# Fewer vector operations between the rank products and the places of routed rows, in a two-layer mixture-of-experts and state-space kernel

## The chip, the cores and the metric

The kernel runs on one core of one Trainium2 chip. The metric is the device time of one execution in microseconds (us). The engines are called by the profile's names: PE (TensorE, matrix products; PEld is its weight loads), DVE (VectorE), ACT (ScalarE), POOL (GpSimd) and SP (SyncE, which here only starts transfers).

## What is computed

1024 rows of width 256 (4 sequences of 256) go through three residual blocks: half a mixture-of-experts (MoE) block, a state-space scan, and half the same MoE block again. The MoE block, cut to what matters:

```python
logits = einsum('th,eh->te', xt, w_router)            # 8 experts
scores = sigmoid(logits)
topk_w, topk_i = top_k(scores, 2)                     # two experts for each row
topk_w = topk_w / sum(topk_w)
comb = zeros((T, 8)).at[arange(T)[:, None], topk_i].add(topk_w)
gate = silu(einsum('th,eih->tei', xt, wg)); up = einsum('th,eih->tei', xt, wu)
expert_out = einsum('tei,ehi->teh', gate * up, wd)    # inner width 640
out = einsum('te,teh->th', comb, expert_out)          # + two shared experts (sg, su, sd) for every row
```

The scan has, for each row, 256 channels and 16 states: `h = exp(dt * A) * h + dt * B * x`, `y = h . C + D * x`. All is float32.

## The kernel before

**Segments.** The rows are cut into two halves of 512. The program has four segments: the first MoE block on half 0 and on half 1 (segments 0 and 1), then the second MoE block on half 0 and on half 1 (2 and 3). The scan of half 0 runs between tiles of segment 1, that of half 1 between tiles of segment 2. Every segment has 17 tiles of 128 rows: 8 of the two shared experts (kind "shared"), 5 "whole" tiles for experts 0 to 4 and 4 "mixed" tiles of four groups of 32 rows: one group whose expert is looked up at run time and three of fixed experts (`MIXED`). A tile is gate and up projections (L510 or L525 on PE), tanh on ACT (L784), two DVE operations (L1031, L1035), the down projection (L535 or L548) and, for a shared tile, its addition to the residual on DVE (L1046, tile `xres`). `first(n)` issues the projections of tile n + 1, `second(n)` the down projection of tile n. The projections have two halves of the accumulators in flight: `rest_of_gate_up(n)` waits on `s_ev` until tile n - 2 has been moved out of PSUM, which for a shared tile is L1046.

**Routing.** Only the two best experts of a row compute it. On DVE `route_scores` finds them as one-hot arrays `one1` and `one2` (4 blocks of 128 rows x 8 experts) and adds them into `both`. PE's `rank` multiplies `both` by a triangular matrix (rank of each row within its block, L602) and by ones (totals of the blocks, L603), into PSUM bank 7. DVE's `route_rows` turns these into places: it sums the totals over earlier blocks (L1147), counts the 32-row groups that an expert needs beyond its own room (L1150 to L1158), adds steps and bases and picks the places of the two experts of every row (L1161 to L1172), and writes them as integers to `pos` (L1173, L1174). POOL then scatters the normalized rows to these places in the DRAM buffer `xg_rows` with eight indirect transfers (L957), four and four: the second four wait until the first four have landed. SP loads tiles from there (L391, into `xg`), and PE turns them (L554) on the way to the first whole tile.

**Order.** One table, `SCHEDULE`, is walked by every engine, and each engine runs its own parts in that order. In segment 0 DVE does `route_scores`, the two operations of tile 0, then `route_rows`, and then the two operations of tile 1; segment 0's first whole tile is number 5, and PE turns its rows while it works on tile 3. In segment 1 the step "scored and ranked" stands among the whole tiles; in segments 2 and 3 it stands between shared tiles (32 and 33 in segment 2). In such a step DVE does `route_scores` and `route_rows` back to back, and only then the operations of the next tile and the L1046 of the present one. `link(...)` makes DVE wait for the result of one operation before the next starts; an operation without it may overlap the next.

## Time and profile before

| | before |
|---|---|
| median of 3 runs | 516.63 us (516.49 to 517.44) |
| profiled execution: time, span | 519.28 us, 517.1 us |
| PE busy, instructions | 504.5 us (98%), 4636 |
| DVE busy, instructions | 323.6 us (63%), 650 |
| ACT / POOL busy | 153.9 us (30%) / 229.0 us (44%) |
| granted TensorE clock, mean | 0.997 |
| chain that ended last | PE 81%, DVE 8%, DMA 6%, issue 2%, POOL 2% |

The span is the stretch of the profiled execution in which instructions are recorded. The profile adds 2.2 us around it, and this execution is 2.65 us above the median of the unprofiled runs. "Idle before" an instruction is what its engine lost just ahead of it, with the one that ended the wait; only waits on PE, or on an engine that PE then waits for, touch the end.

### The profile page before, as it was taken

To read this page: it belongs to the slowest core of one execution; us is meant where nothing else is said; L and a number is where in the kernel's file an instruction comes from. 1 tells how busy PE (TensorE), PEld (TensorE's weight loads), DVE (VectorE), ACT (ScalarE), POOL (GpSimd) and SP (SyncE) were. 2 spreads that over 40 slices of the span, in tenths; PEclk is the share of its full clock that TensorE was granted. 3 is DMA by queue.
4 is the path that set the end of the run, shared out by engine and by line. 5 is a ranking of instruction groups with operands and counts; after the bars stand their busy time and mean duration, and the time that the engine had idled before them with its cause. 6 is when DMAs were issued, how large, how long until landed. Compare 5 with 4: busy or idle time off the path is not lost.

```text
span 517.1 us, 11597 instructions
## 1 busy us (share of the span) xinstructions
PE 504.5 (98%) x4636; PEld 420.3 (81%) x4637; DVE 323.6 (63%) x650; ACT 153.9 (30%) x322; POOL 229.0 (44%) x205
## 2 busy tenths in 40 slices
PE   7998999999999999999989999999999999999997
PEld 6998997568979999557889789975598899955796
DVE  3663328222656999998679399999977532422225
ACT  1111132221145444453112634445521111122210
POOL 1042000602315999997353289999930650000032
PEclk9899999999999999999999999999999999999999
DMA  7956999421415556640121534555100231210012
GB/s 226 388 190 248 398 396 350 144 74 31 122 34 135 135 120 157 132 129 20 52 72 43 126 88 130 143 142 153 56 22 3 72 97 57 82 42 15 19 52 82
DMA packets 39639, 64.36 MB, mean 124 GB/s; under 512 B 4864, under 2 KB 22784, under 8 KB 39584
## 3 DMA queue, kind: packets, MB, share of 16 engines
q1 hardware_dynamic: 27264, 36.98, 25.5%
q10 hardware_dynamic: 9088, 18.09, 9.4%
q0 software_dynamic: 3232, 8.53, 5.3%
q8 instruction: 39, 0.64, 0.5%
q14 instruction: 16, 0.13, 0.1%
HBM read 46.93 MB, written 16.65 MB: 123 GB/s over the span
## 4 chain that ended last, share of the span: by engine, by line
PE 81%; DVE 8%; DMA 6%; issue 2%; POOL 2%; SPq 1%; ACT 0%; DVEq 0%; POOLq 0%
PE ps L510 35%; PE ps L535 19%; PE ps L525 14%; PE ps L548 7%; DMA bcb<-bc_rows 2%; PE ps L559 2%; PE ps L554 2%; DMA w_gu<-in_su 1%; DMA xg_rows<-region,pos 1%; POOL xg_rows L957 1%; DMA bc_rows<-hh 1%; PE ps L702 1%; DVE hb L1031 1%; PE ps L593 1%; SPq L368 1%
## 5 line engine op out<-in xcount | busy, mean ns | idle before, releaser
L510 PEld LDWEIGHTS ps<-xnp,w_gu 128*128 128x128 f32 x1280 | 149.0, 193 | 11.6 <-issue 6.2
L510 PE MATMUL ps<-xnp,w_gu 128*128 128x128 f32 x1280 | 152.8, 278 | 4.7 <-DVE xres L1046 3.7
L1031 DVE SCALAR_TENSOR_TENSOR hb<-hb,ps 128x640 f32<-128x640 f32 x68 | 55.5, 816 | 120.2 <-ACT hb L784 120.0
L535 PE MATMUL ps<-w_dn,hb 128*128 128x256 f32 x520 | 120.9, 380 | 0.0
L535 PEld LDWEIGHTS ps<-w_dn,hb 128*128 128x128 f32 x520 | 95.0, 191 | 10.6
L784 ACT ACTIVATE hb<-ps 128x640 f32<-128x640 f32 x68 | 47.6, 700 | 176.8 <-PE ps L510 163.0
L510 PEld LDWEIGHTS ps<-xt,w_gu 128*128 128x128 f32 x800 | 92.4, 192 | 1.1 <-issue 0.2
L510 PE MATMUL ps<-xt,w_gu 128*128 128x128 f32 x800 | 92.8, 276 | 0.0
L1076 DVE TENSOR_TENSOR_SCAN ps<-ps,region 128x512 f32<-128x512 f32 x64 | 78.3, 1223 | 7.9 <-POOL region L995 6.9
L1009 POOL TENSOR_TENSOR xna<-xna,hh 128x512 f32<-128x512 f32 x64 | 81.9, 1282 | 2.0 <-DVE hh L1081 2.0
L975 POOL DMA_INDIRECT region<-yg_rows,pos x32 | 30.7, 959 | 112.2 <-DMA yg_rows<-ob 92.0
L525 PE MATMUL ps<-w_gu,xt 128*32 128x256 f32 (+2 forms) x1024 | 74.5, 434 | 0.0
L957 POOL DMA_INDIRECT xg_rows<-region,pos x32 | 31.5, 986 | 95.2 <-DMA xg_rows<-bcb 40.2
L995 POOL TENSOR_TENSOR region<-region,bcb 128x512 f32<-128x512 f32 x44 | 56.2, 1279 | 19.3 <-DMA bcb<-bc_rows 16.2
L525 PEld LDWEIGHTS ps<-w_gu,xt 128*32 128x32 f32 x1024 | 31.3, 110 | 36.8 <-issue 23.8
L1035 DVE TENSOR_TENSOR hb<-hb,ps 128x640 f32<-128x640 f32 x68 | 55.8, 821 | 3.5 <-PE ps L510 1.2
L878 ACT ACTIVATE ps<-region,aneg 128x510 f32<-128x510 f32 x64 | 43.3, 677 | 0.0
L548 PE MATMUL ps<-w_dn,hb 128*32 128x256 f32 (+1 forms) x640 | 37.6, 380 | 0.0
L811 ACT ACTIVATE ob<-ps 128x256 f32<-128x256 f32 x36 | 13.8, 383 | 68.5 <-PE ps L548 36.0
L548 PEld LDWEIGHTS ps<-w_dn,hb 128*32 128x32 f32 x640 | 20.4, 110 | 13.6 <-issue 0.7
L1081 DVE TENSOR_TENSOR hh<-ps,bcb 128x512 f32<-128x512 f32 x44 | 30.4, 691 | 1.5
L995 POOL TENSOR_TENSOR region<-region 128x512 f32<-128x512 f32 x20 | 25.6, 1280 | 2.7 <-DVE ps L1076 2.7
(110 smaller groups left out, 281.7 us busy)
## 6 DMA issues: line engine op xcount, KB each, us to landing
bcb<-bc_rows SPq DMA_DIRECT2D x22, 512.0 KB, 5.2
region<-bc_rows SPq DMA_DIRECT2D x10, 512.0 KB, 5.4
w_gu<-in_wg ACTq DMA_DIRECT2D x7, 640.0 KB, 8.6
w_gu<-in_wu ACTq DMA_DIRECT2D x7, 640.0 KB, 10.2
w_dn<-in_wd ACTq DMA_DIRECT2D x7, 640.0 KB, 12.9
xg<-xg_rows SPq DMA_DIRECT2D x20, 128.0 KB, 5.0
yg_rows<-ob SPq DMA_DIRECT2D x20, 128.0 KB, 4.3
xg_rows<-bcb SPq DMA_DIRECT2D x1, 2176.0 KB, 13.7
```

The costliest lines, as they stand in the source:

```text
L510: last = nc.tensor.matmul(gup(p)[:, c * P:(c + 1) * P], w_gu4[:, e, k, c * P:(c + 1) * P], x, start=(k == 0), stop=(k == KC - 1))
L525: last = nc.tensor.matmul(gup(p)[r:r + GROUP, a:b], xt[:, p, k, r:r + GROUP], w, start=(k == 0), stop=(k == KC - 1))
L535: ins = nc.tensor.matmul(outp(p), hb[:, p, c * P:(c + 1) * P], w_dn4[:, e, c, :], start=(c == 0), stop=(c == IC - 1))
L548: ins = nc.tensor.matmul(outp(p)[r:r + GROUP, :], hb[:, p, c * P + r:c * P + r + GROUP], w, start=(c == 0), stop=(c == IC - 1))
L784: nc.scalar.activation(hb[:, p, :], gup(p)[:, 0:I], ACT.Tanh, scale=0.5).then_inc(s_tanh, 1)
L878: nc.scalar.activation(bank[:, :, 1:L], dt[:, d, :].rearrange("p (b t) -> p b t", b=2)[:, :, 1:L], ACT.Exp, scale=aneg[:, d * N + m:d * N ...
L957: nc.gpsimd.indirect_dma_start(out=xg_dram[s % 2], out_offset=bass.IndirectOffsetOnAxis(ap=pos[:, s, j, t:t + 1], axis=0), in_=xn["P"][:, ...
L995: nc.gpsimd.tensor_tensor(bx[:, d, :], dtx[:, d, :], bcs[m % SLOTS][:, 0, :], ALU.mult).then_inc(s_bx, 1)
L1009: nc.gpsimd.tensor_tensor(xna[:, d, :], xna[:, d, :], hh[:, d, :], ALU.add).then_inc(s_acc, 1)
L1031: nc.vector.scalar_tensor_tensor(out=h, in0=h, scalar=1.0, in1=gup(p)[:, 0:I], op0=ALU.add, op1=ALU.mult).then_inc(s_a, 1)
L1035: nc.vector.tensor_tensor(h, h, gup(p)[:, I:GU], ALU.mult).then_inc(s_h, 1)
L1076: nc.vector.tensor_tensor_scan(state_banks[:, d, :], state_banks[:, d, :], bx[:, d, :], 0.0, ALU.mult, ALU.add).then_inc(s_scan, 1)
```

## The change

The places are worked out by fewer and larger operations.

- The rows of one expert now lie in one run of `xg_rows` and `yg_rows`: the tiles are laid out in `ROW_ORDER`, so that an expert's whole tile and its groups in a mixed tile are neighbours (`FIRST_ROW`). The step from the first to the later part of an expert (`STEP`) is gone. The rooms, the number of groups and the size of the buffers are the same.
- The sums over earlier blocks and the base of each expert go into the rank products. `both` becomes 8 x 6: per expert a share of the base (1/128 of it in every partition, written once at the start from `plan`), the four blocks, and a zero. One DVE scan over these 48 elements gives `upto`, the running sums per expert (`carry` is 0 at each expert's first element). PE multiplies ones by `upto` (40 columns) and adds the triangular product of `both` (32 columns) into the same bank; 1 is taken from the whole triangular matrix, so that a block's own total is left out again. `s_oh`, for which PE waits, is given by the scan and no longer by the addition ahead of it.
- `route_rows` reads ranks with bases straight from PSUM. The shift of `cum` by one element replaces a subtraction, `one1` and `one2` lie side by side in `tops` and are multiplied, reduced and converted in one operation each. By the rows below it has 11 DVE operations, where it had 25 (four of them the L1147).
- `s_rkc`, which tells PE that bank 7 may be written again, comes after the eighth of these and no longer after the second.
- `ex` is the same buffer as `sc`. The memory that ACT copies zeros from in the scan is `zero8` and no longer `pre`. The constant `plan` has 80 columns, where it had 40.

The diff, cut to its core:

```diff
@@ -23,8 +23,12 @@
 GROUP = 32
 MIXED = [(5, 5, 5), (0, 0, 2), (1, 1, 3), (6, 6, 7)]
 MT = len(MIXED)
-STATIC0 = WHOLE * P
-FREE0 = STATIC0 + MT * 3 * GROUP
+
+ROW_ORDER = [("whole", 0), ("mixed", 1), ("whole", 2), ("whole", 1), ("mixed", 2), ("whole", 3), ("whole", 4),
+             ("mixed", 0), ("mixed", 3)]
+ROW_OWNERS = [e for kind, k in ROW_ORDER for e in ((k,) * 4 if kind == "whole" else MIXED[k])]
+FIRST_ROW = {tile: GROUP * sum(4 if kind == "whole" else 3 for kind, _ in ROW_ORDER[:k]) for k, tile in enumerate(ROW_ORDER)}
+FREE0 = GROUP * len(ROW_OWNERS)
...
-BASE = [P * e if e < WHOLE else STATIC0 + GROUP * OWN.index(e) for e in range(E)]
-STEP = [STATIC0 + GROUP * OWN.index(e) - P - P * e if e < WHOLE and e in OWN else 0 for e in range(E)]
-OVER = [FREE0 - ROOM[e] - BASE[e] - STEP[e] for e in range(E)]
+BASE = [GROUP * ROW_OWNERS.index(e) for e in range(E)]
+OVER = [FREE0 - ROOM[e] - BASE[e] for e in range(E)]
...
-        plan = sb("plan", [P, 5 * E])
-        room, base, step_on, over_on, room_groups = (plan[:, k * E:(k + 1) * E] for k in range(5))
+        plan = sb("plan", [P, 4 * E + E * (TT + 2)])
+        room_end, over_on, end_groups, base_share = (plan[:, k * E:(k + 1) * E] for k in range(4))
+        carry = plan[:, 4 * E:]
...
-        ex = sb("ex", [P, TT, E])
         sc = sb("sc", [P, TT, E])
+        ex = sc
...
-        one1 = sb("one1", [P, TT, E])
...
-        both = sb("both", [P, TT, E])
-        tot = sb("tot", [P, TT, E])
-        pre = sb("pre", [P, TT + 1, E])
-        nt = sb("nt", [P, E])
-        cum = sb("cum", [P, E])
+        tops = sb("tops", [P, 2, TT, E])
+        one1, one2 = tops[:, 0, :, :], tops[:, 1, :, :]
+
+        both = sb("both", [P, E, TT + 2])
+        upto = sb("upto", [P, E, TT + 2])
+        zero8 = sb("zero8", [P, E])
+        nt = sb("nt", [P, E + 1])
+        cum = sb("cum", [P, E + 1])
...
+        m12 = sb("m12", [P, 2, TT])
+        m1, m2 = m12[:, 0, :], m12[:, 1, :]
@@ -383,11 +388,11 @@
...
-                    a, b = FREE0 + m * GROUP, STATIC0 + m * 3 * GROUP
+                    a, b = FREE0 + m * GROUP, FIRST_ROW["mixed", m]
...
-                    a = m * P
+                    a = FIRST_ROW["whole", m]
@@ -598,10 +604,10 @@
             def rank(s):
                 pe.wait_ge(s_oh, s + 1)
                 banks_free()
-                flat = both[:, :, :].rearrange("p t e -> p (t e)")
-                nc.tensor.matmul(bank7[:, 0:TT * E], upper[:, :], flat, start=True, stop=True)
-                nc.tensor.matmul(bank7[:, TT * E:2 * TT * E], ones[:, :], flat, start=True,
-                                 stop=True).then_inc(s_rk, 1)
+                own = both[:, :, 1:TT + 1].rearrange("p e t -> p t e")
+                sums = upto[:, :, 1:TT + 2].rearrange("p e t -> p t e")
+                nc.tensor.matmul(bank7[:, 0:(TT + 1) * E], ones[:, :], sums, start=True, stop=False)
+                nc.tensor.matmul(bank7[:, 0:TT * E], upper[:, :], own, start=False, stop=True).then_inc(s_rk, 1)
                 held[:] = [(s_rkc, s + 1)]
@@ -874,7 +880,7 @@
...
-                    nc.scalar.activation(bank[:, :, 0:1], pre[:, 0, 0:2].rearrange("p (b t) -> p b t", t=1), ACT.Copy)
+                    nc.scalar.activation(bank[:, :, 0:1], zero8[:, 0:2].rearrange("p (b t) -> p b t", t=1), ACT.Copy)
@@ -1120,65 +1126,60 @@
                 link(nc.vector.tensor_scalar(sc[:, :, :], ex[:, :, :], 1.0, None, ALU.add))
                 link(nc.vector.reciprocal(sc[:, :, :], sc[:, :, :]))
...
-                nc.vector.tensor_tensor(both[:, :, :], one1[:, :, :], one2[:, :, :], ALU.add).then_inc(s_oh, 1)
-
-                link(nc.vector.tensor_tensor(kk[:, :], m1[:, :], m2[:, :], ALU.add))
+                link(nc.vector.tensor_tensor(both[:, :, 1:TT + 1].rearrange("p e t -> p t e"), one1, one2,
+                                             ALU.add))
+
+                nc.vector.tensor_tensor_scan(upto[:, :, :].rearrange("p e t -> p (e t)"), carry,
+                                             both[:, :, :].rearrange("p e t -> p (e t)"), 0.0, ALU.mult,
+                                             ALU.add).then_inc(s_oh, 1)
+
+                link(nc.vector.tensor_tensor(kk[:, :], m1, m2, ALU.add))
...
             def route_rows(s):
 
                 dve.wait_ge(s_rk, s + 1)
-                nc.vector.tensor_copy(eq[:, :, :].rearrange("p t e -> p (t e)"), bank7[:, 0:TT * E])
-                nc.vector.tensor_copy(tot[:, :, :].rearrange("p t e -> p (t e)"),
-                                      bank7[:, TT * E:2 * TT * E]).then_inc(s_rkc, 1)
-                dve.wait_ge(s_rkc, s + 1)
-                for t in range(TT):
-                    link(nc.vector.tensor_tensor(pre[:, t + 1, :], pre[:, t, :], tot[:, t, :], ALU.add))
-
-
-                link(nc.vector.scalar_tensor_tensor(out=nt[:, :], in0=pre[:, TT, :], scalar=1.0 / GROUP,
-                                                    in1=room_groups, op0=ALU.mult, op1=ALU.subtract))
-                link(nc.vector.tensor_tensor(needs, nt[:, :].rearrange("p (e a) -> p e a", a=1)
+                rank = bank7[:, 0:TT * E].rearrange("p (t e) -> p t e", t=TT)
+
+
+                link(nc.vector.scalar_tensor_tensor(out=ebase[:, :], in0=bank7[:, TT * E:(TT + 1) * E], scalar=1.0 / GROUP,
+                                                    in1=end_groups, op0=ALU.mult, op1=ALU.subtract))
+                nc.vector.tensor_tensor(eq[:, :, :], rank, over_t(room_end), ALU.is_ge)
+                link(nc.vector.tensor_tensor(needs, ebase[:, :].rearrange("p (e a) -> p e a", a=1)
                                              .to_broadcast([P, E, STEPS]), slots[:, 0:STEPS].rearrange("p (a c) -> p a c", a=1)
                                              .to_broadcast([P, E, STEPS]), ALU.is_gt))
-                link(nc.vector.tensor_reduce(nt[:, :], needs, AX.X, ALU.add))
-                link(nc.vector.tensor_tensor_scan(cum[:, :], ones[:, 0:E], nt[:, :], 0.0, ALU.mult, ALU.add))
-                link(nc.vector.tensor_tensor(ebase[:, :], cum[:, :], nt[:, :], ALU.subtract))
-                link(nc.vector.scalar_tensor_tensor(out=ebase[:, :], in0=ebase[:, :], scalar=float(GROUP), in1=over_on,
+                link(nc.vector.tensor_reduce(nt[:, 1:E + 1], needs, AX.X, ALU.add))
+                link(nc.vector.tensor_tensor_scan(cum[:, :], ones[:, 0:E + 1], nt[:, :], 0.0, ALU.mult, ALU.add))
+                link(nc.vector.scalar_tensor_tensor(out=ebase[:, :], in0=cum[:, 0:E], scalar=float(GROUP), in1=over_on,
                                                     op0=ALU.mult, op1=ALU.add))
-
-                link(nc.vector.tensor_tensor(eq[:, :, :], eq[:, :, :], pre[:, 0:TT, :], ALU.add))
-                nc.vector.scalar_tensor_tensor(out=sc[:, :, :], in0=eq[:, :, :], scalar=P - 0.5,
-                                               in1=over_t(step_on), op0=ALU.is_gt, op1=ALU.mult)
-                link(nc.vector.tensor_tensor(both[:, :, :], eq[:, :, :], over_t(room), ALU.is_ge))
-                link(nc.vector.tensor_tensor(both[:, :, :], both[:, :, :], over_t(ebase[:, :]), ALU.mult))
-                link(nc.vector.tensor_tensor(eq[:, :, :], eq[:, :, :], sc[:, :, :], ALU.add))
-                link(nc.vector.tensor_tensor(eq[:, :, :], eq[:, :, :], both[:, :, :], ALU.add))
-                link(nc.vector.tensor_tensor(eq[:, :, :], eq[:, :, :], over_t(base), ALU.add))
-                nc.vector.tensor_tensor(one1[:, :, :], one1[:, :, :], eq[:, :, :], ALU.mult)
-                link(nc.vector.tensor_tensor(one2[:, :, :], one2[:, :, :], eq[:, :, :], ALU.mult))
-                nc.vector.tensor_reduce(m1[:, :], one1[:, :, :], AX.X, ALU.add)
-                link(nc.vector.tensor_reduce(m2[:, :], one2[:, :, :], AX.X, ALU.add))
-                nc.vector.tensor_copy(pos[:, s, 0, :], m1[:, :])
-                nc.vector.tensor_copy(pos[:, s, 1, :], m2[:, :]).then_inc(s_dest, 1)
+                link(nc.vector.tensor_tensor(eq[:, :, :], eq[:, :, :], over_t(ebase[:, :]), ALU.mult))
+                nc.vector.tensor_tensor(eq[:, :, :], eq[:, :, :], rank, ALU.add).then_inc(s_rkc, 1)
+                dve.wait_ge(s_rkc, s + 1)
+                link(nc.vector.tensor_tensor(tops[:, :, :, :].rearrange("p j t e -> p j (t e)"),
+                                             tops[:, :, :, :].rearrange("p j t e -> p j (t e)"),
+                                             eq[:, :, :].rearrange("p (a t) e -> p a (t e)", a=1).to_broadcast([P, 2, TT * E]),
+                                             ALU.mult))
+                link(nc.vector.tensor_reduce(m12[:, :, :].rearrange("p j t -> p (j t)"),
+                                             tops[:, :, :, :].rearrange("p j t e -> p (j t) e"), AX.X, ALU.add))
+                nc.vector.tensor_copy(pos[:, s, :, :], m12[:, :, :]).then_inc(s_dest, 1)
 
@@ -1201,7 +1202,9 @@
...
             nc.vector.memset(zeros, 0.0).then_inc(s_zero, 1)
-            nc.vector.memset(pre[:, 0, :], 0.0).then_inc(s_boot, 1)
+            nc.vector.memset(zero8[:, :], 0.0).then_inc(s_boot, 1)
+            nc.vector.memset(nt[:, :], 0.0)
+            nc.vector.memset(both[:, :, :], 0.0)
             link(nc.vector.memset(ones[:, :], 1.0))
             nc.vector.memset(rt[:, :], 0.0).then_inc(s_boot, 1)
@@ -1231,6 +1234,8 @@
                     dve.wait_ge(s_aneg, 1)
                 elif kind == "start":
                     copy_logits(0)
+                    dve.wait_ge(s_cst, 16 * N_CST)
+                    link(nc.vector.tensor_copy(both[:, :, 0], base_share))
                     route_scores(0)
                     hidden(0)
@@ -1302,8 +1307,10 @@
...
-    room_groups = [r // GROUP for r in ROOM]
-    plan = np.concatenate([np.asarray(v, np.float32).ravel() for v in (ROOM, BASE, STEP, OVER, room_groups)])
+    ends = [r + b for r, b in zip(ROOM, BASE)]
+    carry = np.tile([0.0] + [1.0] * (TT + 1), E)
+    plan = np.concatenate([np.asarray(v, np.float32).ravel() for v in
+                           (ends, OVER, [r / GROUP for r in ends], [b / P for b in BASE], carry)])
...
-        "upper": np.triu(np.ones((P, P), np.float32), 1),
+        "upper": np.triu(np.ones((P, P), np.float32), 1) - 1.0,
```

How the instructions stand now, at three places. On DVE, the end of `route_scores` in segment 0 (`one1`, `one2` are the one-hot arrays, `m1`, `m2` the best scores, `kk` a scratch). Before:

```order
L1127 TENSOR_TENSOR one2<-keys,kk 128x32
L1131 TENSOR_TENSOR both<-one1,one2 128x32
L1133 TENSOR_TENSOR kk<-m1,m2 128x4
L1134 RECIPROCAL kk<-kk 128x4
L1135 TENSOR_SCALAR kk<-kk 128x4
L1136 TENSOR_TENSOR wgt<-m1,kk 128x4
```

And of the change (`tops` holds both one-hot arrays, `m12` both scores):

```order
L1133 TENSOR_TENSOR tops<-keys,kk 128x32
L1137 TENSOR_TENSOR both<-tops 128x4x8
L1140 SCALAR_TENSOR_TENSOR upto<-plan,both 128x48
L1144 TENSOR_TENSOR kk<-m12 128x4
L1145 RECIPROCAL kk<-kk 128x4
L1146 TENSOR_SCALAR kk<-kk 128x4
```

A scan has come in between `both` and `kk`, and its result `upto` is what PE now waits for.

Still on DVE, `route_rows` of segment 0, which follows the two operations of tile 0. Its first ten rows before, with the four additions L1147 in one row (`tot` totals of blocks, `pre` sums over earlier blocks, `hh` the comparison with the group counts, `cum` and `ebase` groups given out so far):

```order
L1142 COPY eq<-ps 128x32
L1143 COPY tot<-ps 128x32
L1147 TENSOR_TENSOR pre<-pre,tot 128x8 x4
L1150 SCALAR_TENSOR_TENSOR nt<-pre,plan 128x8
L1152 TENSOR_TENSOR hh<-nt,slots 128x128
L1155 TENSOR_REDUCE nt<-hh 128x8
L1156 SCALAR_TENSOR_TENSOR cum<-ones,nt 128x8
L1157 TENSOR_TENSOR ebase<-cum,nt 128x8
L1158 SCALAR_TENSOR_TENSOR ebase<-ebase,plan 128x8
L1161 TENSOR_TENSOR eq<-eq,pre 128x32
```

The other twelve rows before, up to the places `pos`:

```order
L1162 SCALAR_TENSOR_TENSOR sc<-eq,plan 128x32
L1164 TENSOR_TENSOR both<-eq,plan 128x32
L1165 TENSOR_TENSOR both<-both,ebase 128x32
L1166 TENSOR_TENSOR eq<-eq,sc 128x32
L1167 TENSOR_TENSOR eq<-eq,both 128x32
L1168 TENSOR_TENSOR eq<-eq,plan 128x32
L1169 TENSOR_TENSOR one1<-one1,eq 128x32
L1170 TENSOR_TENSOR one2<-one2,eq 128x32
L1171 TENSOR_REDUCE m1<-one1 128x4
L1172 TENSOR_REDUCE m2<-one2 128x4
L1173 CAST pos<-m1 128x4
L1174 CAST pos<-m2 128x4
```

And the whole of it in the change:

```order
L1156 SCALAR_TENSOR_TENSOR ebase<-ps,plan 128x8
L1158 TENSOR_TENSOR eq<-ps,plan 128x32
L1159 TENSOR_TENSOR hh<-ebase,slots 128x128
L1162 TENSOR_REDUCE nt<-hh 128x8
L1163 SCALAR_TENSOR_TENSOR cum<-ones,nt 128x9
L1164 SCALAR_TENSOR_TENSOR ebase<-cum,plan 128x8
L1166 TENSOR_TENSOR eq<-eq,ebase 128x32
L1167 TENSOR_TENSOR eq<-eq,ps 128x32
L1169 TENSOR_TENSOR tops<-tops,eq 128x64
L1173 TENSOR_REDUCE m12<-tops 128x8
L1175 CAST pos<-m12 128x8
```

The copies out of PSUM, the sums over blocks, the step and base additions and one of each pair at the end are gone; `ebase`, `eq` and `eq` read `ps` themselves.

On PE, the rank products of segment 0, which stand between projections of tile 1 (L510). Before, behind the turned logits (L609):

```order
L609 MATMUL ps<-ident,hh 128x128
L510 MATMUL ps<-xnp,w_gu 128x128 x20
L602 MATMUL ps<-both,upper 128x32
L603 MATMUL ps<-both,ones 128x32
L510 MATMUL ps<-xnp,w_gu 128x128 x12
L535 MATMUL ps<-w_dn,hb 128x256 x5
```

And of the change:

```order
L615 MATMUL ps<-ident,hh 128x128
L516 MATMUL ps<-xnp,w_gu 128x128 x20
L609 MATMUL ps<-upto,ones 128x40
L610 MATMUL ps<-both,upper 128x32
L516 MATMUL ps<-xnp,w_gu 128x128 x12
L541 MATMUL ps<-w_dn,hb 128x256 x5
```

The two products have changed places, and the one with ones has 40 columns, where it had 32; around them PE's order is the same.

## Rows read from the trace of the kernel before

**Rows 1.** Waits of PE: who waited for whom, us in total, times, longest.

```profile
PE ps L510 <- DVE xres L1046: 3.7, 4, 1.2
PE ps L554 <- DMA xg<-xg_rows: 1.4, 1, 1.4
PE ps L602 <- DVE both L1131: 1.0, 3, 0.3
PE ps L510 <- DMA w_gu<-in_su: 1.0, 1, 1.0
```

**Rows 2.** Timeline of PE, segment 0: start us, us, operation, idle before.

```profile
30.24 2.32 PE L535 MATMUL ps<-w_dn,hb 128*128 128x256 f32 x10
...
36.87 2.33 PE L535 MATMUL ps<-w_dn,hb 128*128 128x256 f32 x10
...
45.09 0.41 PE L554 MATMUL ps<-ident,xg 128*128 128x128 f32 x2 [1.44 <-DMA xg<-xg_rows]
45.34 2.32 PE L535 MATMUL ps<-w_dn,hb 128*128 128x256 f32 x10
...
52.18 2.33 PE L535 MATMUL ps<-w_dn,hb 128*128 128x256 f32 x10
```

**Rows 3.** The chain that ended last, segment 0: start us, us, what.

```profile
32.27 4.11 DMA xg_rows<-region,pos
...
40.46 2.41 DMA xg_rows<-region,pos
42.89 2.06 DMA xg<-xg_rows
```

**Rows 4.** Timeline of DVE, segment 0: the last operation of the places.

```profile
27.12 0.16 DVE L1174 CAST pos<-m 128x4 int32<-128x4 f32 x1
```

**Rows 5.** Windows; the last two columns are DMA share and GB/s.

```profile
28.00:30.00 2.00, 2.00 (x19) 2.00 (x19) 1.90 (x6) 0.46 (x1) 1.47 (x2) 1.00 0.98 387
30.00:32.00 2.00, 2.00 (x13) 1.80 (x12) 1.85 (x4) 0.25 (x1) 1.66 (x2) 1.00 0.51 198
```

**Rows 6.** Timeline of PE, the routing steps of segments 2 and 3.

```profile
260.19 0.41 PE L602 MATMUL ps<-both,upper 128*128 128x32 f32 x2 [0.35 <-DVE both L1131]
...
260.66 2.40 PE L535 MATMUL ps<-w_dn,hb 128*128 128x256 f32 x10
...
267.83 1.16 PE L510 MATMUL ps<-xnp,w_gu 128*128 128x128 f32 x8 [1.19 <-DVE xres L1046]
268.82 2.33 PE L535 MATMUL ps<-w_dn,hb 128*128 128x256 f32 x10
...
403.71 1.16 PE L510 MATMUL ps<-xnp,w_gu 128*128 128x128 f32 x8 [1.19 <-DVE xres L1046]
```

**Rows 7.** Timeline of DVE, the routing step of segment 2.

```profile
259.95 0.19 DVE L1131 TENSOR_TENSOR both<-one 128x32 f32<-128x32 f32 x1
...
260.93 0.19 DVE L1142 COPY eq<-ps 128x32 f32<-128x32 f32 x1
...
265.70 0.16 DVE L1174 CAST pos<-m 128x4 int32<-128x4 f32 x1
...
267.36 0.42 DVE L1046 SCALAR_TENSOR_TENSOR xres<-ps,xres 128x256 f32<-128x256 f32 x1
```

**Rows 8.** Groups of DVE instructions: form, count, busy us, mean ns of one, idle before.

```profile
L1076 DVE TENSOR_TENSOR_SCAN ps<-ps,region 128x512 f32<-128x512 f32 x64 | 78.3, 1223 | 7.9 <-POOL region L995 6.9 <-ACT ps L878 1.0
...
L1147 DVE TENSOR_TENSOR pre<-pre,tot 128x8 f32<-128x8 f32 x16 | 2.7, 167 | 0.5
...
L1152 DVE TENSOR_TENSOR hh<-nt,slots 128x128 f32<-128x128 f32 x4 | 1.2, 291 | 0.1
...
L1156 DVE TENSOR_TENSOR_SCAN cum<-ones,nt 128x8 f32<-128x8 f32 x4 | 0.7, 174 | 0.1
```

**Rows 9.** Tile w_gu until 120 us: durations, first and last start; then all its landings.

```profile
L525 PE MATMUL ps<-w_gu,xt x256: 378/379/617, 84.6 to 111.5; 128*32 x64, 128*32 128x256 f32 x48, 128*32 128x512 f32 x16
...
L779 ACTq DMA_DIRECT2D w_gu<-in_wu x7: 619/632/644, 43.6 to 66.9; - x7
...
DMA to landing us min/median/max: 5.2/8.9/12.8
```

More of the change, by code:

```diff
@@ L398, in store_rows @@
                 if kind_of(n) == "mixed":
-                    a, b = FREE0 + m * GROUP, STATIC0 + m * 3 * GROUP
+                    a, b = FREE0 + m * GROUP, FIRST_ROW["mixed", m]
                     sp.dma_start(rows[a:a + GROUP, :], ob[0:GROUP, q, :]).then_inc(s_y[q], 16)
@@ L402, in store_rows @@
                 else:
-                    sp.dma_start(rows[m * P:(m + 1) * P, :], ob[:, q, :]).then_inc(s_y[q], 16)
+                    a = FIRST_ROW["whole", m]
+                    sp.dma_start(rows[a:a + P, :], ob[:, q, :]).then_inc(s_y[q], 16)
             def fetch_rows(m):
@@ L1122, in route_scores @@
                 for top, one in ((m1, one1), (m2, one2)):
-                    link(nc.vector.tensor_reduce(top[:, :], sc[:, :, :], AX.X, ALU.max))
-                    link(nc.vector.tensor_tensor(eq[:, :, :], sc[:, :, :], over_e(top[:, :]), ALU.is_equal))
+                    link(nc.vector.tensor_reduce(top, sc[:, :, :], AX.X, ALU.max))
+                    link(nc.vector.tensor_tensor(eq[:, :, :], sc[:, :, :], over_e(top), ALU.is_equal))
                     link(nc.vector.tensor_tensor(eq[:, :, :], eq[:, :, :], keys[:, :, :], ALU.mult))
@@ L1126, in route_scores @@
                     link(nc.vector.tensor_reduce(kk[:, :], eq[:, :, :], AX.X, ALU.max))
-                    link(nc.vector.tensor_tensor(one[:, :, :], keys[:, :, :], over_e(kk[:, :]), ALU.is_equal))
+                    link(nc.vector.tensor_tensor(one, keys[:, :, :], over_e(kk[:, :]), ALU.is_equal))
                     if one is one1:
-                        link(nc.vector.scalar_tensor_tensor(out=sc[:, :, :], in0=one[:, :, :], scalar=-2.0,
+                        link(nc.vector.scalar_tensor_tensor(out=sc[:, :, :], in0=one, scalar=-2.0,
@@ L1134, in route_scores @@
+                link(nc.vector.tensor_tensor(kk[:, :], m1, m2, ALU.add))
                 link(nc.vector.reciprocal(kk[:, :], kk[:, :]))
                 link(nc.vector.tensor_scalar(kk[:, :], kk[:, :], 0.25, None, ALU.mult))
-                nc.vector.tensor_tensor(wgt[:, s, 0, :], m1[:, :], kk[:, :], ALU.mult)
-                link(nc.vector.tensor_tensor(wgt[:, s, 1, :], m2[:, :], kk[:, :], ALU.mult))
+                nc.vector.tensor_tensor(wgt[:, s, 0, :], m1, kk[:, :], ALU.mult)
+                link(nc.vector.tensor_tensor(wgt[:, s, 1, :], m2, kk[:, :], ALU.mult))
@@ L1178, in overflow_table @@
                     over, slots[:, :].rearrange("p (j a) -> p j a", a=1).to_broadcast([P, GROUPS_MAX, E]),
-                    over_t(cum[:, :], GROUPS_MAX), ALU.is_ge))
+                    over_t(cum[:, 1:E + 1], GROUPS_MAX), ALU.is_ge))
                 link(nc.vector.tensor_reduce(tf[:, :], over, AX.X, ALU.add))
-                nc.vector.tensor_scalar(limit[0:1, s:s + 1], cum[0:1, E - 1:E], float(-MT), 0.0, ALU.add, ALU.max)
+                nc.vector.tensor_scalar(limit[0:1, s:s + 1], cum[0:1, E:E + 1], float(-MT), 0.0, ALU.add, ALU.max)
                 nc.vector.tensor_scalar(table[0:1, s % 2 * GROUPS_MAX:(s % 2 + 1) * GROUPS_MAX], tf[0:1, :],
```

3 lines of the change are left out of this document (removed).

## Prediction

> **What bounds the kernel now.** I read four views in this order. The page's busy shares say that PE works 98% of the span, so a shorter vector chain pays only where PE stands still for it. The waits of PE name such places [rows 1]: four waits for the eviction L1046 (3.7 us), one of 1.4 us for the first routed rows, three of 0.3 us for `both`. The timelines of PE and DVE say which of these hang on the routing chain. Last, the chain that ended last says what lies between the places and the first routed rows. The reader should see three kinds of place.
>
> Segment 0: PE waits 1.44 us at 45.09 for `xg` [rows 2]. The period from one down projection to the next is 45.34 - 36.87 = 8.47 us there, and one period later, with the same turning of rows in it and no wait, 52.18 - 45.34 = 6.84 [rows 2]. The stall is thus 1.63 us. Behind it stand the places, ready at 27.12 + 0.16 = 27.28 [rows 4], two lots of four scatters, of which the last landings are at 36.38 and 42.87, and the load, landed at 44.95 [rows 3].
>
> Segments 2 and 3: DVE does all routing ahead of the eviction of the tile that PE has finished. The eviction ends at 267.78 [rows 7], and PE, which waited 1.19 us, goes on at 267.83; segment 3 shows the same 1.19 [rows 6]. The period here is 268.82 - 260.66 = 8.16 [rows 6] against 36.87 - 30.24 = 6.63 for a shared tile without a wait [rows 2], an excess of 1.53. The stall is between 1.19 and 1.53; I take 1.4, nearer to the period, since the first matmuls after a wait run longer than their like and the profile's wait leaves that out. The other two of the four L1046 waits belong to the starts of the scans (3.7 less 2 x 1.19 leaves 1.3 us for both), where no routing is near; they stay.
>
> Segments 1 to 3: PE waits 0.3 us each for `both` at the rank products [rows 1, 6]. In segment 0 it doesn't.
>
> **The scan that is added.** A scan of 8 elements takes 174 ns and one of 512 takes 1223 [rows 8], so 2.08 ns for an element more and 174 + 40 x 2.08 = 257 ns for 48. Small linked operations stand a little apart: L1147's 16 had 0.5 us of idle time ahead of them, 30 ns each at most [rows 8]; I take 22. So `s_oh`, and with it PE's rank products and all that DVE does behind, come 0.28 us later. Segments 1, 2 and 3 pay this on PE, since PE waits there already. In segment 0 the products stand between projections and PE arrives later than `both`; I count nothing, and 0.28 if that cover is gone.
>
> **The chain that is cut.** `route_rows` took from 260.93 to 265.86, 4.93 us for 25 operations [rows 7]. The new one I build from sizes: 8 elements cost 167 ns and 128 cost 291 [rows 8], 1.03 ns for an element, so 32 cost 192 and 64 cost 225. With 22 ns behind each linked one: first `ebase` 0.19; the comparison of 32, which the next operation overlaps, 0.11, the middle between nothing and 0.21; comparison and reduction of 128, 0.31 each; scan of 9, 0.20; `ebase` 0.19; two of 32, 0.21 each; one of 64, 0.25; its reduction 0.24; conversion of 8, 0.17. The sum is 2.39 us. The chain is 4.93 - 2.39 = 2.54 shorter, and the places are ready 2.54 - 0.28 = 2.26 us earlier. No row shows a two-input operation that takes its small operand straight from PSUM, but the copy L1142 does read PSUM and took 0.19 like others of its size [rows 7], so I add nothing; at twice the price for three of them it is 0.55 more, and 1.7 us are still saved.
>
> **Segments 2 and 3.** The eviction, at 267.78 now, comes at 265.5. PE wants to go on at 267.83 - 1.4 + 0.28 = 266.7. So the wait is gone with 1.2 us to spare; it would come back only if the saving were under 1.1 us. Each gives 1.4 - 0.28 = 1.12, both 2.24. What is late next is nothing: PE finds the following hidden values done too, as DVE's two operations of tile 33 come 2.3 us earlier.
>
> **Segment 0.** If all moves by 2.26, the load lands at 42.7, and PE wants it at 45.09 - 1.63 = 43.5: the wait of 1.63 is gone with 0.8 to spare. Between lie transfers whose length may change. The first four scatters would start near 26 and lie wholly in the weight traffic, which fills the DMA engines to 0.98 until 30 and to 0.51 until 32 [rows 5]. From issue to landing the fourth took 4.11 and the eighth, in quiet, 2.41 [rows 3]. The first four carry 4 x 128 KB, 1.3 us at the 387 GB/s of that stretch [rows 5]. Bounds: the first lot lands 2.26 earlier, or not earlier at all (36.38 again). The fourth would be issued at 30.0, in the ebbing traffic, as it is now, so I take the full shift. It needs 1.5 of the 2.26 to remove the wait. The load then also no longer starts at the moment in which ACT issues the next experts' weights.
>
> Will the 1.63 us hold? Weights are sent as PE goes on, over a DMA that is full. The last `in_wu` send is at 66.9 and the longest landing of `w_gu` 12.8, so 79.7 at worst, while the first mixed tile, which wants them all, starts at 84.6, or 83.0 when moved [rows 9]. 3.3 us remain.
>
> **Small parts.** The order of the rows in DRAM leaves transfers of the same number and size. The clearing of `zero8`, `nt` and `both` puts two short memsets ahead of PE's warm-up, and `plan` is 20 KB larger; PE waits 1.0 us for shared weights after the warm-up [rows 1], which covers the first, and 20 KB at 387 GB/s is 0.05. The copy of the base share stands where DVE waits for the turned logits. The later `s_rkc` holds bank 7 longer by about 1.5 us, but PE's next use of it is tiles away. `ex` in `sc`: same operations, same sizes, nothing. All these 0, at most 0.1.
>
> The rank products have 72 columns, where they had 64. A down projection has 2560 columns in 2.16 us (its ten instructions), 0.84 ns for a column, and each product goes twice: 16 x 0.84 = 0.01 us. Their moving operands now step by 24 bytes. No row shows such a read. Low bound nothing; high bound four times the price, 144 columns x 0.84 x 3 = 0.36 us in each of three segments. I take the low one, since only 72 columns are read. On this the Trainium skill (SBUF, "Door 1: The DMA port swizzle") says that SBUF is read in lines of 16 bytes and that every access which crosses to a new line "pays a penalty", here every element. It gives no price. Doubled, by its rule, the sum would be 0.12 x 3 = 0.36 us worse; by the rows it is unchanged.
>
> **Sum.** -1.63 + 0.28 - 2.24 = -3.59 us. The span goes from 517.1 to 513.5, the profiled time from 519.28 to 515.7, the median from 516.63 to 513.0.
>
> **Rivals.**
> - A, the scatter of segment 0 doesn't move: its first lot lands when the weight traffic lets it, near 36.4, and PE still waits there. For it: the 4.11 against 2.41, and the 0.98. Against it: the fourth landed over 4 us after the traffic had ebbed, and its issue is what moves. Sum 0.28 - 2.24 = -1.96, 514.7. Chance 0.13.
> - B, nothing to be measured: the PSUM reads and the broadcast products cost so much that the chain saves less than 1.1 us, and rank comes 0.28 later three times. Then the stalls shrink by some 0.3 each and the delay eats it: 516.3. Against it: 14 operations fewer at 0.2 each. Chance 0.04.
> - C, slower: the strided moving operands. PE reads 144 columns in a step, and it stands still for them in segments 1 to 3. To end 1.03 us above the median they must eat 3.59 + 1.03 in three places, 1.5 us each, 10 ns for a column against 0.84. At that price 517.8. Chance 0.03.
> - Otherwise the forecast, 0.8.
>
> **Range.** The forecast's own: the stalls of 1.19 or 1.53 move it by 0.4 and 0.3, the strided reads by up to 1.1 upward, the run-to-run spread by 0.3: 512.4 to 514.2. With A it ends at 514.8. A measurement can tell about 0.2% (1.03 us) from no change. Faster takes the forecast and A, 0.93; same is B, 0.04; slower C, 0.03.
>
> **What would show it.** Right: the wait of PE for `xg` is gone or under 0.1; PE's waits for L1046 fall from four to two, 1.3 us in all; those for `both` become waits for `upto`, of 0.6 us; `route_rows` takes 2.4 us, and the places of segment 0 are ready near 25.0; the first scatter lot lands near 34.1. Wrong: a wait for `xg` near 43.5 (A), `upto` waits above 0.8, rank products longer than 0.47 us from the first to the next work (C), or a new wait on weights between 45 and 85 us.

## The result, and the profile after

The changed kernel takes 513.64 us (median of 7 runs, 512.51 to 515.68) against 517.23 for the kernel before, run beside it (516.49 to 518.47): 3.6 us less, a ratio of 0.9931 with a 95% interval of 0.9906 to 0.9956. The forecast was -3.59, 513.0. Twelve further runs (`e5`) gave a ratio of 0.9933 (0.9908 to 0.9958). The profiled execution's time is 513.58, its span 511.6, thus 5.5 less than the one of before; 1.7 of that has nothing to do with the change, as shown below.

The page's head of the changed kernel:

```profile
span 511.6 us, 11548 instructions
...
PE 502.6 (98%) x4636; PEld 418.7 (82%) x4637; DVE 317.0 (62%) x601; ACT 153.6 (30%) x322; POOL 228.9 (45%) x205
```

DVE has 49 instructions fewer in the span and is 6.6 us less busy; PE has the same number. The waits of PE say where that counts:

```profile
PE ps L609 <- DVE upto L1140: 2.0, 3, 0.7
PE ps L697 <- DVE rt L1211: 1.8, 1, 1.8
PE ps L516 <- DVE xres L1052: 1.1, 2, 0.7
PE ps L516 <- DMA w_gu<-in_su: 0.8, 1, 0.8
```

Read beside [rows 1]: the wait for `xg` is gone, the four for the eviction (now L1052) are two, those at the starts of the scans, and the three for `both` are three for `upto`, twice as long. The timeline of PE in segment 0, the counterpart of [rows 2], has the period with the first turned rows at 42.04 - 35.20 = 6.84 us:

```profile
35.20 2.32 PE L541 MATMUL ps<-w_dn,hb 128*128 128x256 f32 x10
37.36 4.63 PE L516 MATMUL ps<-xnp,w_gu 128*128 128x128 f32 x40
41.82 0.38 PE L560 MATMUL ps<-ident,xg 128*128 128x128 f32 x2
42.04 2.32 PE L541 MATMUL ps<-w_dn,hb 128*128 128x256 f32 x10
```

In segment 2 (counterpart of [rows 6]) PE waits longer ahead of the rank products, and no longer behind them; the shared tile's period is 264.64 - 257.94 = 6.70, where it was 8.16:

```profile
257.47 0.43 PE L609 MATMUL ps<-upto,ones 128*128 128x40 f32 x2 [0.65 <-DVE upto L1140]
257.71 0.40 PE L610 MATMUL ps<-both,upper 128*128 128x32 f32 x2
257.94 2.40 PE L541 MATMUL ps<-w_dn,hb 128*128 128x256 f32 x10
260.18 4.63 PE L516 MATMUL ps<-xnp,w_gu 128*128 128x128 f32 x40
264.64 2.33 PE L541 MATMUL ps<-w_dn,hb 128*128 128x256 f32 x10
```

DVE there, counterpart of [rows 7]: from 258.28 to 260.77 the places take 2.49 us, where they took 4.93, and the eviction ends at 262.68, while PE wants it near 263.75 (32 of its 40 matmuls behind 260.18; from there to 264.64 they take 0.1115 us each), 1.07 later.

```profile
258.28 0.17 DVE L1156 SCALAR_TENSOR_TENSOR ebase<-ps,plan 128x8 f32<-128x8 f32 x1
...
260.60 0.17 DVE L1175 CAST pos<-m 128x8 int32<-128x8 f32 x1
...
262.26 0.42 DVE L1052 SCALAR_TENSOR_TENSOR xres<-ps,xres 128x256 f32<-128x256 f32 x1
```

And the groups of DVE instructions, counterpart of [rows 8]: the last number ahead of the second bar is the mean of one in ns.

```profile
L1140 DVE TENSOR_TENSOR_SCAN upto<-plan,both 128x48 f32<-128x48 f32 x4 | 1.0, 257 | 0.1
...
L1169 DVE TENSOR_TENSOR tops<-tops,eq 128x64 f32<-128x64 f32 x4 | 0.9, 224 | 0.1
...
L1137 DVE TENSOR_TENSOR both<-tops 128x32 f32<-128x32 f32 x4 | 0.9, 216 | 0.1
...
L1156 DVE SCALAR_TENSOR_TENSOR ebase<-ps,plan 128x8 f32<-128x8 f32 x4 | 0.7, 164 | 0.2
```

**Stretches, not spans.** A stretch between two of PE's own steps leaves the start of the execution out. Each routing step begins with the router's products (`wr`, L593, now L599); segments 1 and 2 then reach the scan's projections (`wx`, L725, now L731), and segment 3 the last group of down projections. In the trace of before:

```profile
75.84 0.64 PE L593 MATMUL ps<-xnp,wr 128*32 128x128 f32 x16
...
149.56 0.65 PE L725 MATMUL ps<-xna,wx 128*32 128x128 f32 x16
...
254.43 0.65 PE L593 MATMUL ps<-xnp,wr 128*32 128x128 f32 x16
...
285.20 0.65 PE L725 MATMUL ps<-xna,wx 128*32 128x128 f32 x16
...
390.32 0.65 PE L593 MATMUL ps<-xnp,wr 128*32 128x128 f32 x16
...
509.41 4.48 PE L535 MATMUL ps<-w_dn,hb 128*128 128x256 f32 x20
```

And after:

```profile
72.64 0.65 PE L599 MATMUL ps<-xnp,wr 128*32 128x128 f32 x16
...
146.69 0.64 PE L731 MATMUL ps<-xna,wx 128*32 128x128 f32 x16
...
251.41 0.64 PE L599 MATMUL ps<-xnp,wr 128*32 128x128 f32 x16
...
281.02 0.64 PE L731 MATMUL ps<-xna,wx 128*32 128x128 f32 x16
...
385.99 0.65 PE L599 MATMUL ps<-xnp,wr 128*32 128x128 f32 x16
...
503.94 4.48 PE L541 MATMUL ps<-w_dn,hb 128*128 128x256 f32 x20
```

Segment 1: 73.72 before, 74.05 after, +0.33. Segment 2: 30.77 and 29.61, -1.16. Segment 3: 119.09 and 117.95, -1.14. The forecast had +0.28, -1.12 and -1.12. The two stretches between these, with the scans, are 104.87 and 105.12 before and 104.72 and 104.97 after. In the eleven profiles below they lie anywhere from 104.3 to 105.6, whatever the kernel, so their 0.3 us is not counted for the change.

**The start.** The windows of the kernel before (the third number from the end is PE's granted clock) show a stretch at half the clock, that is at 1.2 GHz, which begins half a microsecond behind the end of its wait for the shared weights:

```profile
12.00:13.00 1.00, 1.00 (x8) 0.96 (x6) 0.00 (x0) 0.00 (x0) 0.00 (x0) 0.59 0.99 358
13.00:14.00 1.00, 1.00 (x18) 0.60 (x16) 0.00 (x0) 0.00 (x0) 0.00 (x0) 0.50 1.07 386
14.00:15.00 1.00, 1.00 (x11) 0.81 (x4) 0.29 (x1) 0.00 (x0) 0.00 (x0) 0.50 1.08 385
15.00:16.00 1.00, 1.00 (x8) 1.00 (x8) 0.00 (x0) 0.00 (x0) 0.00 (x0) 0.71 1.08 386
```

The missing shares add up to 0.41 + 0.5 + 0.5 + 0.29 = 1.7 us. The changed kernel's profiled execution has 1.00 in these windows. But it comes and goes with the execution: the profiles of `e2`, `e4`, `e6` and `e10` below have such a stretch too, those of the others don't. The mean clock of an execution, which doesn't say where it fell, was 0.999 or 1.0 in 25 of 29 runs of before on one chip and less in four; of the first 7 runs of the changed kernel it was so in five and two. So 1.7 of the 5.5 us between the spans is the start. The change's own effect is better read from the medians, 3.6 apart, and from the stretches.

### The profile page after: what moved, and what is told of

The parts are those of the page before. It is cut to its first block, busy times and chain, and to the rows that moved or that the text cites. A ratio compares the mean times of both kernels' runs of the same rounds, so it can differ in the third digit from the quotient of the medians.

```text
span 511.6 us, 11548 instructions
## 1 busy us (share of the span) xinstructions
PE 502.6 (98%) x4636; PEld 418.7 (82%) x4637; DVE 317.0 (62%) x601; ACT 153.6 (30%) x322; POOL 228.9 (45%) x205
## 4 chain that ended last, share of the span: by engine, by line
PE 89%; DMA 5%; DVE 3%; issue 1%; SPq 1%; POOL 0%; ACT 0%; DVEq 0%; POOLq 0%
PE ps L516 41%; PE ps L541 21%; PE ps L531 14%; PE ps L554 7%; DMA bcb<-bc_rows 2%; PE ps L565 2%; PE ps L560 2%; DMA w_gu<-in_su 1%; DMA bc_rows<-hh 1%; PE ps L708 1%; SPq L373 1%; POOL region L1001 0%; DVE ps L1082 0%; PE ps L599 0%; PE ps L749 0%
## 5 line engine op out<-in xcount | busy, mean ns | idle before, releaser
L516 PE MATMUL ps<-xnp,w_gu 128*128 128x128 f32 x1280 | 151.1, 276 | 1.8 <-DVE xres L1052 1.1
L1041 DVE TENSOR_TENSOR hb<-hb,ps 128x640 f32<-128x640 f32 x68 | 55.8, 821 | 2.3
```

Of the source, the lines that this page charges most:

```text
L516: last = nc.tensor.matmul(gup(p)[:, c * P:(c + 1) * P], w_gu4[:, e, k, c * P:(c + 1) * P], x, start=(k == 0), stop=(k == KC - 1))
L1041: nc.vector.tensor_tensor(h, h, gup(p)[:, I:GU], ALU.mult).then_inc(s_h, 1)
```

## The experiments

Eleven kernels, on three chips; each is compared with runs of the kernel before on its own chip.

**Does segment 0 count?** `e1_pad_seg0` lengthens the new chain again, in segment 0 alone:

```diff
+                for _ in range(11 if s in (0,) else 0):
+                    link(nc.vector.tensor_tensor(tf[:, :], slots[:, :], slots[:, :], ALU.mult))
                 nc.vector.tensor_copy(pos[:, s, :, :], m12[:, :, :]).then_inc(s_dest, 1)
```

> The changed kernel with eleven linked copies-like operations of 30 elements (0.21 us each, 2.3 us) ahead of the last conversion, in segment 0 alone. Theory (the shorter chain gains because the first routed rows arrive in time): PE waits again for xg, 1.4 to 2.0 us, and some 1.7 us of the 3.6 are lost: 1.9 us under the kernel before. Rival (what is gained lies in segments 2 and 3 alone, segment 0 was covered by transfers): no wait on xg, still 3.6 us under before.

516.09 us against 517.09 for before, ratio 0.999 (0.9977 to 1.0004). PE waits where it did before:

```profile
44.05 0.41 PE L560 MATMUL ps<-ident,xg 128*128 128x128 f32 x2 [1.63 <-DVE hb L1041]
```

The row names DVE as releaser, since its L1041 ended at 44.03. But that operation makes the hidden values of the next tile, and in the kernel before PE turned the rows at 45.09 while the same operation ran until 45.27. What PE waits for is the load of `xg`: it was issued at 41.85 and landed 2.1 us later, and PE goes on 0.1 behind it, as in the kernel before. So PE waits again, and the rival is out. From router to router the profile has 62.11 us (12.68 to 74.79), 1.6 to 2.1 more than two profiles of the changed kernel (60.49 and 60.02, below). By the medians more was lost than the 1.7 expected, 2.6 us of the 3.6. Part of that is the clock: six of the 12 runs had a mean clock under 0.999. The other six have a median of 515.8, and the 25 such runs of before 517.07, so that 2.3 of 3.6 are lost. The interval, 0.7 us either way, covers the rest.

**Do segments 2 and 3 count, and from what length on?** `e2_pad_seg23` has the same edit with `(2, 3)`, `e8_pad_small` has five of the operations there instead of eleven.

> The same eleven operations in segments 2 and 3 alone. Theory: the eviction L1052 has 1.1 us to spare in the changed kernel, so 2.3 us of padding bring back some 1.25 us of wait in each of two segments: 2.5 us lost, 1.1 us under before, and PE's waits for xres are four again. Rival (the gain is from somewhere else, such as the layout or the start): still 3.6 us under before.

> The changed kernel with five of the padding operations, 1.05 us, in segments 2 and 3. Theory: the eviction has 1.07 us to spare, so nothing is lost, at most 0.2 us of wait in each. Rival (each DVE operation costs PE its length): 2.1 us slower than the changed kernel.

`e2`: 516.7 against 517.09, ratio 0.9987 (0.9964 to 1.0011). The eviction is waited for again, in both places:

```profile
266.61 1.16 PE L516 MATMUL ps<-xnp,w_gu 128*128 128x128 f32 x8 [1.24 <-DVE xres L1052]
...
402.88 1.16 PE L516 MATMUL ps<-xnp,w_gu 128*128 128x128 f32 x8 [1.24 <-DVE xres L1052]
```

3.2 of the 3.6 us are lost, where 2.5 were expected. The stretches say the same: segment 2 takes 31.19 us (252.79 to 283.98) and segment 3 119.45 (389.13 to 508.58), 1.58 and 1.50 more than after the change, for waits of 1.24. `e8`: 513.77, ratio 0.9914 (0.9882 to 0.9947), against 513.42 for the changed kernel on the same chip: 0.35 us for 2.1 us of added DVE work. Neither eviction is listed as waited for in its trace; the one of segment 2 ends at 263.70, just when PE wants it, and the two stretches are some 0.15 us longer each (29.76 and 118.11). So DVE's work costs next to nothing until the slack of 1.07 is used up, and somewhat more than its length beyond: in `e2` some 2.4 us were added in each segment, 1.35 more than the slack.

**Is it the layout?** `e9_layout_only` is the kernel before with `ROW_ORDER` and `FIRST_ROW`, and

```diff
+BASE = [GROUP * ROW_OWNERS.index(e) for e in range(E)]
+STEP = [0] * E
```

> The kernel before with the new order of the rows in DRAM and nothing else (its 25 operations still run, with a step of zero). Theory (the layout changes no transfer's number or size): as the kernel before, within 0.4 us. Rival (neighbouring rows make the scatters or loads cheaper, and a part of the gain comes from that): the wait for xg in segment 0 shorter by 0.5 us or more, and faster by as much.

517.08 against 516.9, ratio 1.0001 (0.9977 to 1.0025); the wait for `xg` is there, 1.34 us. The layout by itself is worth nothing that can be seen: the interval is 1.2 us either way, and the stretches of segments 1, 2 and 3 are 73.73, 30.77 and 119.10, within 0.01 of before. This execution had the full clock at the start, so it is the fairer witness for segment 0:

```profile
13.19 0.64 PE L596 MATMUL ps<-xnp,wr 128*32 128x128 f32 x16
...
74.66 0.65 PE L596 MATMUL ps<-xnp,wr 128*32 128x128 f32 x16
```

61.47 us from router to router. The changed kernel's first profile has 60.02 (12.62 to 72.64), a gain of 1.45.

**The yardstick.** `e5_after_again` is the changed kernel on the chip of e6 to e8.

> The changed kernel, unchanged, as the yardstick on the chip of the next three. Both theories: 3.0 to 3.8 us under the kernel before.

513.42 against 517.04, 3.6 us less. In its trace a piece of the wait is left:

```profile
41.66 0.41 PE L560 MATMUL ps<-ident,xg 128*128 128x128 f32 x2 [0.37 <-DMA xg<-xg_rows]
```

The stretch from router to router is 60.49 here (11.92 to 72.41), a gain of 0.98 on the 61.47 of e9. Why a wait is left here and not in the first profile, POOL's timeline shows. In the first profile the fourth scatter was issued at 28.50 and had landed at 33.06, 0.27 ahead of the fifth's start at 33.33. In `e5` everything runs 0.7 us earlier, the places (22.82) and the fourth scatter too, but the lot lands no earlier, at 33.04:

```profile
27.81 0.97 POOL L963 DMA_INDIRECT xg_rows<-region,pos  x1 [0.31 <-issue]
33.31 0.97 POOL L963 DMA_INDIRECT xg_rows<-region,pos  x1 [4.53 <-DMA xg_rows<-region,pos]
```

And in `e10`, where it was issued 3.4 us later than here, it landed only 0.6 us later:

```profile
31.20 0.97 POOL L965 DMA_INDIRECT xg_rows<-region,pos  x1 [0.30 <-issue]
33.89 0.97 POOL L965 DMA_INDIRECT xg_rows<-region,pos  x1 [1.72 <-DMA xg_rows<-region,pos]
```

In all eight profiles of kernels with the short chain and no padding in segment 0 the fourth scatter was issued between 27.8 and 31.2 and landed between 33.0 and 34.0. The DMA engines are busy to over 0.9, above all with weights, until 31 in the profile of `e5`, to 0.45 until 32 and to 0.05 in the microsecond behind that. So here the landing goes with the end of that traffic and no longer with the places, and PE waits when its own start was early: 0.37 us in `e5`, 0.31 in `e8`, 0.58 in `e11`, nothing where its router began at 12.6 or later.

**Is it the number of operations, or where they stand?** The places can also be worked out behind the eviction. `e3_rank_behind` and `e4_before_behind` change `SCHEDULE` in the changed kernel and in the kernel before:

```diff
-("scored and ranked", 8, 1), ("second", 8), ("decay",)
+("scored", 8, 1), ("second", 8), ("R2", 1), ("decay",)
-("scored and ranked", S1 + 15, 2), ("S", 2, 0), ("second", S1 + 15)
+("scored", S1 + 15, 2), ("second", S1 + 15), ("R2", 2), ("S", 2, 0)
-("scored and ranked", S2 + 16, 3), ("S", 3, 0), ("S", 3, 1), ("second", S2 + 16)
+("scored", S2 + 16, 3), ("second", S2 + 16), ("R2", 3), ("S", 3, 0), ("S", 3, 1)
```

> The changed kernel with the rank products and the places of segments 1 to 3 put behind the down projection of the tile, on PE and DVE alike. Theory: PE no longer waits for upto (three waits of 0.66 us) and DVE evicts ahead of the places, so that no wait takes their place: 2.0 to 2.3 us faster than the changed kernel, 5.6 to 5.9 under before. Rival: the places, now later by 2.2 us and ahead of the next tile's two operations, delay those and PE waits there: no faster than the changed kernel.

> The kernel before, with its 25 operations, and only the order of e3. Theory (in segments 2 and 3 it is not the number of operations that costs, but that the eviction stands behind them): the waits of 1.45 twice and of 0.35 three times are gone, 3.9 us under before, with PE's wait for xg in segment 0 left at 1.4. Rival (DVE's total work there decides): only the three waits for both are gone, 1.0 us under before.

`e3`: 511.6 against 517.09, ratio 0.9894 (0.9877 to 0.9912), 5.5 under before. `e4` missed: 518.6, ratio 1.001 (0.9985 to 1.0036). Its waits of segments 1 and 2 are gone, but segment 3 has only four shared tiles ahead of its first whole tile, and with a chain of 4.93 us put behind the down projection the rows come 4.1 us late. The segment takes 123.96 us (386.65 to 510.61), 4.9 more than before, where segments 1 and 2 gave 2.7. Its PE timeline, and the windows behind it:

```profile
416.51 0.66 PE L554 MATMUL ps<-ident,xg 128*128 128x128 f32 x2 [4.12 <-DMA xg<-xg_rows]
```

```profile
416.00:418.00 2.00, 1.49 (x5) 1.34 (x6) 0.00 (x0) 0.38 (x1) 1.38 (x3) 0.50 0.42 128
418.00:420.00 2.00, 2.00 (x7) 1.55 (x6) 0.00 (x0) 0.00 (x0) 1.70 (x2) 0.50 0.59 180
420.00:422.00 2.00, 2.00 (x9) 1.73 (x8) 0.42 (x1) 0.00 (x0) 0.04 (x1) 0.54 0.27 82
```

Behind the idle stretch PE works for over 5 us with the clock at its lower level, 1.2 GHz, which costs it some 2.7 of them. Eleven of the 12 runs of `e4` had a mean clock under 0.999; the one without took 515.63. In `e3` the rows of segment 3 came only 0.89 us late.

`e6_behind_1_and_2` and `e7_before_behind_1_and_2` leave segment 3 as it was: they have the first two of the three pairs of lines of the diff alone.

> The order of e3 in segments 1 and 2 alone; segment 3 keeps the places ahead, since in e3 its first routed rows came 0.9 us late for PE. Theory: the waits for upto of segments 1 and 2 are gone (0.66 each, with what the start after a wait costs some 0.7), that of segment 3 stays, and the wait for xg of 0.9 is gone: 1.4 us faster than the changed kernel and 0.2 us faster than e3. Rival (the start of the scan of half 1 takes back in its wait for xres what segment 2 gains): 0.7 us faster than the changed kernel.

> The kernel before with the order of e3 in segments 1 and 2 alone. Theory (in e4 the later places of segment 3 cost 4.1 us of waiting for xg and a stretch at half the clock behind it, while segments 1 and 2 gained): 0.35 + 0.35 + 1.45, 2.1 us under the kernel before, with segment 3's wait for xres of 1.2 left and no wait for xg there. Rival (25 operations cost PE wherever they stand): no faster than before.

`e6`: 511.54 against 517.04, ratio 0.9882 (0.9842 to 0.9922), 1.9 us faster than `e5`, where 1.4 was expected. `e7`: 513.95, ratio 0.9942 (0.9917 to 0.9968), 3.1 faster than before, where 2.1 was expected. The order alone, with all 25 operations, is thus worth nearly as much as the change. In the stretch of segment 2 of `e6`

```profile
251.97 0.64 PE L599 MATMUL ps<-xnp,wr 128*32 128x128 f32 x16
...
280.67 0.64 PE L731 MATMUL ps<-xna,wx 128*32 128x128 f32 x16
```

28.70 us pass, 0.91 less than after the change, though the wait taken away was 0.65. Segment 1 is 73.10, 0.95 less for a wait of 0.66. The two make the 1.9 of `e6`. `e7` has 28.70 as well (251.50 to 280.20), and 73.08 in segment 1, together 2.7 of its 3.1 us. With no wait left, the number of operations makes no difference.

**The scan on PE's path.** `e10_split_wait` lets the triangular product run under the scan, `e11_split_and_behind` joins that with `e6`:

```diff
-                nc.tensor.matmul(bank7[:, 0:(TT + 1) * E], ones[:, :], sums, start=True, stop=False)
-                nc.tensor.matmul(bank7[:, 0:TT * E], upper[:, :], own, start=False, stop=True).then_inc(s_rk, 1)
+                nc.tensor.matmul(bank7[:, 0:(TT + 1) * E], upper[:, :], own, start=True, stop=False)
+                pe.wait_ge(s_oh, s + 1)
+                nc.tensor.matmul(bank7[:, 0:(TT + 1) * E], ones[:, :], sums, start=False, stop=True).then_inc(s_rk, 1)
```

(`own` has five columns for an expert, and `both` gives a semaphore of its own, for which PE waits ahead of the first product.)

> The changed kernel with the triangular product first, on 40 columns and behind a semaphore of the addition, and the product with ones behind the scan. Theory (the scan of 0.26 us and its link stand on PE's path in segments 1 to 3): the triangular product of 0.24 us runs under the scan, the stretches with a routing step get 0.2 to 0.3 us shorter, 0.7 us faster than the changed kernel in all. Rival (PE pays for the wait as such and not for its length): within 0.2 us of the changed kernel.

> e10 with the order of e6 (places of segments 1 and 2 behind the down projection). Theory: 0.2 to 0.3 us faster than e6, since only segment 3 still waits for the scan: 2.1 to 2.3 us faster than the changed kernel. Rival (as for e10): as e6.

```profile
259.84 0.43 PE L610 MATMUL ps<-both,upper 128*128 128x40 f32 x2 [0.36 <-DVE both L1139]
260.13 0.43 PE L612 MATMUL ps<-upto,ones 128*128 128x40 f32 x2
260.37 1.97 PE L542 MATMUL ps<-w_dn,hb 128*128 128x256 f32 x8
```

The wait is 0.36 again, and segment 2's stretch is 29.40 us (254.06 to 283.46), 0.21 shorter than after the change; those of segments 1 and 3 are 73.81 and 117.74, 0.24 and 0.21 shorter. The time doesn't settle it: `e10` 513.35 against 516.9, ratio 0.9924 (0.9903 to 0.9945), for 0.9933 of the changed kernel on another chip; `e11` 511.4, ratio 0.9904 (0.9878 to 0.993). 0.2 us in each of three stretches is shown, 0.7 in the whole isn't. The fastest versions are `e6` and `e11`, 5.5 us under before, 1.9 under the change.

## Why the prediction was right

- *What bounds the kernel.* Right. PE has the same work, and the time went where its waits went. The waits that forecast and trace share are those for `xg`, the evictions and `upto`.
- *The added scan, 257 ns.* Measured 257. PE's waits became 0.66 for the forecast 0.6, and segment 1's stretch 0.33 longer for 0.28. What was left out is a piece of `both`: its write, now in steps of 24 bytes, takes 216 ns.
- *The cut chain, 2.39 us.* Measured 2.49; sizes of 64 elements at 224 ns (225 forecast), and the small operand from PSUM at 164 ns costs no more than one from SBUF. Adding nothing for PSUM was right.
- *Segments 2 and 3, -1.12 each.* -1.16 and -1.14. Taking 1.4 for the stall, above the profile's wait of 1.19, was needed: by 1.19 they would be -0.91. The spare time of 1.2 is 1.07, and `e8` and `e2` lie on its two sides.
- *Segment 0, -1.63.* The mechanism held (`e1`), the size is -1.0 to -1.5, by execution, and the spare 0.8 us is the number that failed: 0.2 was left in the first profile (load issued at 39.58, landed 2.0 later, turned at 41.82), none in `e5`. The step "so I take the full shift" was too good. Seen from PE, whose down projection began at 28.57 and no longer at 30.24, the places came 2.09 us earlier, for the 2.26 forecast; in absolute time they were ready at 23.52 in the trace after (L1175 of segment 0, 23.35 + 0.17), but the fourth scatter, issued at 28.50, landed only at 33.06, 4.6 us later, where it had been 4.11 [rows 3]. POOL's timeline shows the wait for it:

```profile
28.50 0.97 POOL L963 DMA_INDIRECT xg_rows<-region,pos  x1 [0.30 <-issue]
33.33 0.97 POOL L963 DMA_INDIRECT xg_rows<-region,pos  x1 [3.85 <-DMA xg_rows<-region,pos]
```

  That took back 0.5 us of the shift. It is rival A's mechanism with a better outcome: by the traces the first lot lands when the weight traffic lets it, at 33.04 or 33.06 whether it was issued at 27.81 (`e5`) or at 28.50. Seen from PE's down projection this is 1.65 us earlier than before in the first profile and 0.98 in `e5`, where the wait asks for 1.5 to 1.6. That it came so near was luck and not reckoning. By this a still shorter chain would bring nothing more in segment 0; no run tried one, and none changed the weight traffic.
- *Strided moving operands, nothing.* The two rank products take 257.94 - 257.47 = 0.47 us from the first's start to the next work, as before (260.66 - 260.19) [rows 6], with 8 columns more. Rival C is out for PE, and the rule of the Trainium skill (SBUF, "Door 1: The DMA port swizzle"), that an access which crosses to a new 16-byte line pays a penalty, shows in PE's time not at all. It gives no price; the doubling in the prediction was an assumption. (Rival C's time, by its own figures 516.63 + 1.03, is 517.7 and not 517.8.) On DVE the strided write may show it, with 25 ns over the 191 ns that the same form took when it was dense, on 32 elements.
- *Small parts, layout and buffer.* `e9` has the layout at 1.0001. The longer hold of bank 7, `plan` and the memsets leave no wait of PE, and none on weights appeared between 45 and 85 us. The shared buffer `ex` was not tried alone; in the trace ACT and DVE take the same times around it.
- *The sum.* +0.33, -1.16, -1.14 and -1.0 to -1.5 make -3.0 to -3.4; the forecast was -3.59, and the medians differ by 3.6, with an interval from 2.3 to 4.9. The four terms are borne out each by its own stretch; that forecast and medians agree to 0.01 us is chance.
